# A gated-delta-net layer on one core: the decay matrix from loaded rows, and the products with ones widened from 1 to 64 columns

## The chip, the core and the metric

One core of a Trainium2 chip runs the whole program. The metric is the device time of one execution in microseconds (us). Engines: PE (TensorE) multiplies, DVE (VectorE), ACT (ScalarE) and POOL (GpSimd) do elementwise work, and the queue of SP (SyncE) issues the loop's transfers.

## The reference, cut to what matters

`x` is (8, 1024, 128). A layer norm is followed by an attention-like recurrence over 16 heads, and then by a small feed-forward layer; both are added to `x`.

```
q, k, v = causal_conv_silu(x @ Wq.T), ... ; q, k = l2_norm(q), l2_norm(k)
alpha = exp(-exp(A_log) * softplus(x @ Wa.T + dt_bias));  beta = 2 * sigmoid(x @ Wb.T)
S = alpha_t * (S - beta_t * k_t k_t^T S) + k_t v_t^T;     o_t = S^T q_t     (scan over t)
y = rms_norm(o) @ Wo.T
```

## The kernel before

**Tiling.** The scan is done in chunks of C = 64 positions. One *step* is one pair of heads and one chunk for all 8 batch rows: 8 pairs times 16 chunks, 128 steps. Data of two heads lie on partitions 0 to 63 and 64 to 127, and the 8 rows side by side, so most tiles are 128 x 512. In a chunk, with g the log decay and G its running sum, every product of position t with position j carries the decay exp(G_t - G_j). For one step it stands in `ex` as two 128 x 512 blocks: the one for the Gram matrix of k (multiplied by a column `bn` in `pool_dmn`, L995) and the one for q against k (masked in `pool_dmp`, L999). It is made thus: `pool_lm` (L967) multiplies two triangular masks by g into `Lm`; `pe_dec` (L513) sums them with triangular ones into PSUM; `act_exp` (L726) takes one exponential of 128 x 1024.

**Products with ones.** Three sums over partitions are done on PE with a moving operand of one column: `pe_nk` (L523, squares of k), `pe_nq` (L533, squares of q), `pe_ms` (L696, squares of the output `osq`). PE issues each f32 matmul as two passes, so the trace counts twice as many. In the form column, 64*64 is the part of the array that a pass uses (rows*columns); passes on different parts can run side by side.

**Pipeline.** One turn of the loop works on three steps: n (projections, convolution, decay, Gram matrix), m = n - 1 (inverse of the chunk's triangular system, via DRAM and small blocks), l = n - 2 (output and state). Each engine has its order written by hand (`pe_body`, `act_body`, `dve_body`, `pool_body`, `sp_body`), and semaphores join them. PSUM banks 0 and 1 serve all four projections of a step, so these are a ring: projection on PE (L502), first tap on ACT (L719), three more taps on DVE (L852), then the next projection may start.

**The chain between the second and the third projection.** PE does `pe_gram_p` (L554), `pe_ks` (L626), `pe_dec` (L513), then `pe_ms` (L696), which waits for DVE's PT (L897) because it shares its banks. DVE takes the result in `dve_ro_in` (L881, tile `sc`), PE then does `pe_nk` (L523), DVE `dve_n2` and `dve_r2` (L859, L867), POOL `bn` (L976) and `pool_dmn` (L995), DVE `dve_n` (L890, tile `Nd`), and after that the taps of the third projection (L852). `dve_nqs` (L873) runs once at the end of a step on DVE, so its starts mark the steps.

**Transfers.** SP's queue is in order. In one turn it stores `Nd` to DRAM (`sp_gram`, L1089), waits for these stores, gathers 16 x 16 blocks of it (`sp_gram_in`, L1096, tile `NS`) for POOL's elimination (L1047 and after), and later loads the rows of exp(G) for the query (`sp_g`, L1082, tile `ex`).

Of the kernel before, what the change touches and what calls it, by code (L numbers as in the profile page):

```python
# [14 lines left out]
F32 = mybir.dt.float32  # L15
ALU = mybir.AluOpType
# [23 lines left out]
RESET = -1.0e4  # L40
# [40 lines left out]
def build(nc, x, wtab, wo, wab, hcol, cst, wf, mu, out):  # L81
    with ExitStack() as ctx:
# [18 lines left out]
        Lm = sb("Lm", 2 * 512)  # L101
# [22 lines left out]
        scrG = nc.dram_tensor("scrG", (STEPS, 2, NB * C), F32, kind="Internal").ap()  # L124
        eps = sb("eps", 4)
# [56 lines left out]
        with nc.Block() as block:  # L182
# [32 lines left out]
            def _(dve):  # L215
# [55 lines left out]
                nc.vector.tensor_copy(tp[:, :, 0:8], v8(la))  # L271
                nc.vector.tensor_scalar(tp[:, :, 8:16], v8(be), -1.0, None, ALU.mult)
                dve.wait_ge(cexp.sem, 1)
                nc.vector.scalar_tensor_tensor(tr[:, :, 0:4], v8(tmp[0])[:, :, 0:4], -1.0, v8(be)[:, :, 0:4], ALU.mult, ALU.mult)
                dve.wait_ge(cexp.sem, 2)
                nc.vector.scalar_tensor_tensor(tr[:, :, 4:8], tr[:, :, 4:8], -1.0, v8(be)[:, :, 4:8], ALU.mult, ALU.mult)
# [170 lines left out]
        PB = {"dec": 4, "nk": 2, "gk": 2, "nq": 4, "gp": 2, "ktr": 4, "vtr": 4, "y0": 4, "z0": 4, "x": 2, "y1": 4, "z1": 6, "ks": 6, "u": 2, "o": 2, "ds": 6, "ms": 2, "wo": 6}  # L447
# [635 lines left out]

        def sp_gram(sp, n):
# [552 lines left out]
```

## Time and profile before

| | |
|---|---|
| runs (us) | 3733.55, 3722.45, 3717.49; median 3722.45 |
| profiled execution | span 3725.1 us; no device time beside its span is listed |
| busy: PE, DVE, ACT, POOL | 88%, 70%, 72%, 62% of the span |
| DMA | 28.8% of 16 engines, 61 GB/s |
| mean granted TensorE clock | 0.922 |
| first and last start of L873 | 147.3 and 3505.9 us (128 of them) |
| ahead of the loop: transposes L1379 | 1.95 us for 8 passes, then two PSUM copies L1368 of 0.60 us, then two stores to `scrG` |

The span of the profiled execution lies 2.7 us above the median of the runs. The busy shares are means over the program. The granted clock is given as a share of 2.4 GHz: 1.00 is 2.4 GHz, 0.50 is 1.2 GHz.

### The profile page before, as it was taken

How to read it: one execution, taken by the hardware profiler on the slowest of the kernel's cores; microseconds unless marked ns; L12 is line 12 of the kernel's file. 1: busy time of each engine (PE TensorE's matmuls, PEld its weight loads, DVE VectorE, ACT ScalarE, POOL GpSimd, SP SyncE). 2: the span in 40 equal slices, each digit the busy share in tenths (PEclk: the TensorE clock that was granted, in tenths of full speed). 3: DMA queues.
4: the chain of work that ended last, by engine and by line, in shares of the span. 5: the costliest groups of instructions: out<-in, count | busy, mean ns of one | idle time of the engine just before them, and what ended most of it. 6: DMA issues, size and time to landing. Idle time of an engine off the chain costs nothing. (4 is left out here: it accounts for less than half of the span.)

```text
span 3725.1 us, 195058 instructions
## 1 busy us (share of the span) xinstructions
PE 3292.6 (88%) x77978; PEld 2742.6 (74%) x77978; DVE 2605.8 (70%) x5465; ACT 2677.6 (72%) x5548; POOL 2301.4 (62%) x3558
## 2 busy tenths in 40 slices
PE   5699999999999999999999999999999999999775
PEld 4577777777777777777777777777777777777643
DVE  6677777777777777777777777777777777777453
ACT  2577777777777777777777777777777777777553
POOL 2456666666666666666666666666666666666345
PEclk9789999999999999999999999999999999999777
DMA  2223223232323232323323232323233232323111
GB/s 59 52 61 64 62 62 67 57 67 56 69 56 70 58 66 58 66 59 64 64 60 64 60 67 57 71 57 67 61 63 64 60 65 59 65 59 70 42 34 46
DMA packets 911057, 226.12 MB, mean 61 GB/s; under 512 B 820128, under 2 KB 894112, under 8 KB 911008
## 3 DMA queue, kind: packets, MB, share of 16 engines
q1 hardware_dynamic: 910848, 224.91, 28.8%
q8 instruction: 33, 0.54, 0.1%
q0 software_dynamic: 160, 0.53, 0.0%
q14 instruction: 16, 0.13, 0.0%
HBM read 169.73 MB, written 55.58 MB: 60 GB/s over the span
## 5 line engine op out<-in xcount | busy, mean ns | idle before, releaser
L852 DVE SCALAR_TENSOR_TENSOR cv<-ps,w_kq,cv 128x512 f32<-128x512 f32 x768 | 575.5, 749 | 417.1 <-ACT cv L719 403.5
L852 DVE SCALAR_TENSOR_TENSOR cv<-ps,w_v,cv 128x512 f32<-128x512 f32 x768 | 575.4, 749 | 153.0 <-ACT cv L719 134.9
L1016 POOL TENSOR_TENSOR accT<-accT,X 128x512 f32 (+1 forms) x128 | 163.3, 1276 | 530.2 <-ACT Y L817 530.2
L502 PE MATMUL ps<-xnT,w_kq 128*128 (+1 forms) x1024 | 325.7, 442 | 74.6 <-DVE cv L852 69.0
L502 PE MATMUL ps<-xnT,w_v 128*128 (+1 forms) x1024 | 335.2, 453 | 15.2 <-DVE cv L852 15.0
L1007 POOL TENSOR_TENSOR Sg<-S,tabR 128x512 f32<-128x512 f32 x256 | 333.8, 1323 | 0.0
L976 POOL TENSOR_TENSOR sc<-tabP,sc 128x8 f32<-128x8 f32 x128 | 26.3, 206 | 497.5 <-DVE sc L867 497.5
L765 ACT ACTIVATE Vt<-ps,sc 128x128 f32<-128x128 f32 x1024 | 278.8, 384 | 54.8 <-PE ps L571 54.8
L706 PE MATMUL ps<-wo_s,oo 128*128 128x128 f32 x2048 | 305.6, 309 | 1.2 <-issue 1.2
L967 POOL TENSOR_TENSOR Lm<-k_all,tabP 128x512 f32<-128x512 f32 x256 | 277.2, 1102 | 30.5 <-POOLq L182 30.5
L706 PEld LDWEIGHTS ps<-wo_s,oo 128*128 128x128 f32 x2048 | 280.8, 220 | 14.5 <-issue 1.7
L952 DVE SCALAR_TENSOR_TENSOR Rr<-ps,sc,Vt 128x128 f32<-128x128 f32 x1024 | 288.2, 344 | 1.3
L696 PEld LDWEIGHTS ps<-k_all,KB 128*128 128x128 f32 x2048 | 240.6, 193 | 58.7 <-issue 58.7
L637 PEld LDWEIGHTS ps<-Rr,Z 64*64 64x64 f32 x4096 | 238.1, 141 | 54.5 <-issue 54.5
L502 PEld LDWEIGHTS ps<-xnT,w_kq 128*128 128x128 f32 x1024 | 184.1, 200 | 126.0 <-issue 93.2
L637 PE MATMUL ps<-Rr,Z 64*64 64x128 f32 x4096 | 269.1, 284 | 1.9 <-issue 1.9
L696 PE MATMUL ps<-k_all,KB 128*128 128x1 f32 x2048 | 248.3, 251 | 5.9 <-ACT KB L802 2.1
L585 PEld LDWEIGHTS ps<-Z,NM 64*64 64x64 f32 x8192 | 187.4, 166 | 78.6 <-issue 78.6
L808 ACT ACTIVATE oo<-ps 128x1024 f32<-128x1024 f32 x128 | 131.2, 1025 | 154.3 <-PE ps L653 154.3
L585 PE MATMUL ps<-Z,NM 64*64 64x64 f32 x8192 | 213.2, 255 | 29.2 <-DVE Z L941 28.1
L653 PE MATMUL ps<-PT,U 64*64 64x64 f32 x8192 | 216.7, 221 | 23.8 <-PE ps L650 22.8
L719 ACT ACTIVATE cv<-ps,w_kq 128x512 f32<-128x512 f32 x256 | 174.3, 681 | 74.8 <-PE ps L502 74.7
(197 smaller groups left out, 8542.9 us busy)
## 6 DMA issues: line engine op xcount, KB each, us to landing
ex<-scrG SPq DMA_DIRECT2D x256, 128.0 KB, 2.9
scrN<-Nd SPq DMA_DIRECT2D x256, 128.0 KB, 2.6
Z<-scrZ SPq DMA_DIRECT2D x256, 128.0 KB, 3.2
X<-scrX SPq DMA_DIRECT2D x512, 64.0 KB
w_kq<-wtab SPq DMA_DIRECT2D x128, 132.0 KB, 2.2
w_v<-wtab SPq DMA_DIRECT2D x128, 132.0 KB, 2.5
wo_s<-wo SPq DMA_DIRECT2D x128, 128.0 KB, 2.8
NS<-scrN SPq DMA_DIRECT2D x128, 64.0 KB, 2.6
```

Source lines behind the costliest of these rows:

```text
L502: last = nc.tensor.matmul(pj[:, 4 * g:4 * g + 4, 0:CW], w[:, (j % 2) * P:(j % 2 + 1) * P], xnT3[:, 4 * g:4 * g + 4, bass.ds((n % NC) * C, ...
L585: last = nc.tensor.matmul(ps[place(cls, a), col64(PB["y1" if l else "y0"], cls, i)], blk64(BD["NM"], b, a), blk64(BD["Z"], b, a), start=Tr ...
L637: last = nc.tensor.matmul(ps[a:z, col128(PB["u"], g, i)], blk64(BD["Z"], b, a), unit(Rr, b)[a:z], start=True, stop=True)
L653: last = nc.tensor.matmul(o_cols(h ^ cls, b, d), U[a:z, b * P + d:b * P + d + 64], blk64(BD["PT"], b, a), start=False, stop=(b == NB - 1))
L696: last = nc.tensor.matmul(ps[:, (PB["ms"] + h) * 512 + i:(PB["ms"] + h) * 512 + i + 1], osq[:, h * 512 + i * P:h * 512 + (i + 1) * P], kc( ...
L706: last = nc.tensor.matmul(ps[:, col128(PB["wo"], h, i)], oo[:, h * 512 + i * P:h * 512 + (i + 1) * P], wo_s[:, h * D:(h + 1) * D], start=T ...
L719: nc.scalar.activation(cv4[:, j], pj[:, :, 0:C], ACT.Copy, scale=tap(j, 0)).then_inc(tap0[j].sem, 1)
L765: last = nc.scalar.activation(unit(Vt, b), unit(ps, 4 * PB["vtr"] + b), ACT.Copy, scale=rv[:, b:b + 1])
L852: nc.vector.scalar_tensor_tensor(cv4[:, j], pj[:, :, k:k + C], tap(j, k), cv4[:, j], ALU.mult, ALU.add).then_inc(conv[j].sem, 1)
L952: last = nc.vector.scalar_tensor_tensor(unit(Rr, b), ps[:, col128(PB["ks"], g, i)], cr[:, b:b + 1], unit(Vt, b), ALU.mult, ALU.add)
L967: last = nc.gpsimd.tensor_tensor(v3(Lm, i), over(kc(o, C), NB, C), tabP3[:, bass.ds(n, 1), 0:8].rearrange("p o b -> p b o").to_broadcast([ ...
L1007: nc.gpsimd.tensor_tensor(half(Sg, g).rearrange("p (b v) -> p b v", b=4), half(S, g).rearrange("p (b v) -> p b v", b=4), gam, ALU.mult).th ...
```

## The change

The decay is no longer summed on PE. G itself is kept in `tabP` (rows 0 to 7 of a step) and, transposed, in DRAM (`scrE`, stored once ahead of the loop beside `scrG`). In each turn SP loads the rows G_j, spread over 64 partitions, into `Er` (two transfers of 128 KB, `sp_e`), between `sp_gram` and `sp_gram_in`. POOL subtracts G_t (`pool_df`), ACT takes the absolute value and then exp(-x) of 128 x 512 in `Ee` (`act_abs`, `act_exp`), and POOL makes both blocks of `ex` from the one `Ee`; the masks drop the wrong half as before. The large negative number that cut off the state at a sequence's start is replaced by zeros in the tables `tabR` and `tmp[0]`. The three products with ones move 64 columns (64 equal results, of which the first is read), in blocks of 64 output partitions: `pe_nq` and `pe_ms` become 16 matmuls where they were 8.

```diff
-                la4 = la[:].rearrange("p (h c b) -> p h c b", h=HP, c=NC)
-                nc.vector.memset(la4[0:1, :, 0, :], RESET)
-                then(nc.vector.memset(la4[64:65, :, 0, :], RESET))
...
-        def pe_dec(pe, n):
-            pe.wait_ge(lm_ok.sem, lm_ok.at(n))
-            pe.sem_inc(pe_go.sem, 1)
-            for i, o in enumerate((K_LE, K_GT)):
-                for cls in range(2):
-                    for a, z in HALF:
-                        c = (PB["dec"] + cls) * 512 + i * 4 * C
-                        last = nc.tensor.matmul(ps[place(cls, a), c:c + 4 * C], k_all[a:z, o + a:o + z],
-                                                Lm[a:z, i * 512 + cls * 4 * C:i * 512 + (cls + 1) * 4 * C], start=True, stop=True)
-            last.then_inc(dec_mm.sem, 1)
-
         def pe_nk(pe, n):
             pe.wait_ge(sq_k.sem, sq_k.at(n))
             pe.sem_inc(pe_go.sem, 1)
             for i in range(4):
                 for cls in range(2):
                     for a, z in HALF:
-                        last = nc.tensor.matmul(ps[place(cls, a), (PB["nk"] + cls) * 512 + i:(PB["nk"] + cls) * 512 + i + 1],
-                                                blk64(sq_kt, CLASSES[cls][i], a), k_all[a:z, K_BD + a:K_BD + a + 1],
-                                                start=True, stop=True)
+                        last = nc.tensor.matmul(ps[place(cls, a), col64(PB["nk"], cls, i)], blk64(sq_kt, CLASSES[cls][i], a),
+                                                k_all[a:z, K_BD + a:K_BD + z], start=True, stop=True)
...
-                    last = nc.tensor.matmul(ps[:, (PB["nq"] + h) * 512 + i:(PB["nq"] + h) * 512 + i + 1],
-                                            sq_qt[a:z, i * P:(i + 1) * P], k_all[a:z, K_BD + a:K_BD + a + 1], start=True, stop=True)
+                    for e, (c, d) in enumerate(HALF):
+                        last = nc.tensor.matmul(ps[c:d, col64(PB["nq"], h, i)], blk64(sq_qt, 2 * i + e, a),
+                                                k_all[a:z, K_BD + a:K_BD + z], start=True, stop=True)
...
-            for h in range(2):
-                for i in range(4):
-                    last = nc.tensor.matmul(ps[:, (PB["ms"] + h) * 512 + i:(PB["ms"] + h) * 512 + i + 1],
-                                            osq[:, h * 512 + i * P:h * 512 + (i + 1) * P], kc(K_ONE, 1), start=True, stop=True)
+            for i in range(4):
+                for h in range(2):
+                    for e, (c, d) in enumerate(HALF):
+                        o = h * 512 + (2 * i + e) * C
+                        last = nc.tensor.matmul(ps[c:d, col64(PB["ms"], h, i)], osq[:, o:o + C], kc(K_ONE, C), start=True, stop=True)
...
+        def act_abs(act, n):
+            act.wait_ge(df_ok.sem, df_ok.at(n))
+            if not first(n):
+                act.wait_ge(dmn_ok.sem, dmn_ok.at(n - 1))
+                act.wait_ge(dmp_ok.sem, dmp_ok.at(n - 1))
+            nc.scalar.activation(Ee[:], Er[:], ACT.Abs).then_inc(ab_ok.sem, 1)
+
         def act_exp(act, n):
-            act.wait_ge(dec_mm.sem, dec_mm.at(n))
-            if not first(n):
-                act.wait_ge(nd_ok.sem, nd_ok.at(n - 1))
-                act.wait_ge(pt_ok.sem, pt_ok.at(n - 1))
-            nc.scalar.activation(ex[:, 0:1024].rearrange("p (i g n) -> p g i n", i=2, g=2),
-                                 bank(PB["dec"], 2).rearrange("p (g i n) -> p g i n", g=2, i=2), ACT.Exp).then_inc(dec_ex.sem, 1)
+            act.wait_ge(ab_ok.sem, ab_ok.at(n))
+            nc.scalar.activation(Ee[:], Ee[:], ACT.Exp, scale=-1.0).then_inc(dec_ex.sem, 1)
...
-        def pool_lm(pool, n):
-            if not first(n):
-                pool.wait_ge(dec_mm.sem, dec_mm.at(n - 1))
+        def pool_df(pool, n):
+            pool.wait_ge(e_in.sem, e_in.at(n))
             pool.sem_inc(pool_go.sem, 1)
-            for i, o in enumerate((K_MGT, K_MLE)):
-                last = nc.gpsimd.tensor_tensor(v3(Lm, i), over(kc(o, C), NB, C),
-                                               tabP3[:, bass.ds(n, 1), 0:8].rearrange("p o b -> p b o").to_broadcast([P, NB, C]), ALU.mult)
-            last.then_inc(lm_ok.sem, 1)
+            nc.gpsimd.tensor_tensor(v3(Er, 0), v3(Er, 0), tabP3[:, bass.ds(n, 1), 0:8].rearrange("p o b -> p b o").to_broadcast([P, NB, C]),
+                                    ALU.subtract).then_inc(df_ok.sem, 1)
...
-            nc.gpsimd.tensor_tensor(v3(ex, 0), v3(ex, 0), bcast(bn, C), ALU.mult).then_inc(dmn_ok.sem, 1)
+            if not first(n):
+                pool.wait_ge(nd_ok.sem, nd_ok.at(n - 1))
+            nc.gpsimd.tensor_tensor(v3(ex, 0), v3(Ee, 0), bcast(bn, C), ALU.mult).then_inc(dmn_ok.sem, 1)
 
         def pool_dmp(pool, n):
             pool.wait_ge(dec_ex.sem, dec_ex.at(n))
-            nc.gpsimd.tensor_tensor(v3(ex, 1), v3(ex, 1), over(kc(K_MLE, C), NB, C), ALU.mult).then_inc(dmp_ok.sem, 1)
+            if not first(n):
+                pool.wait_ge(pt_ok.sem, pt_ok.at(n - 1))
+            nc.gpsimd.tensor_tensor(v3(ex, 1), v3(Ee, 0), over(kc(K_MLE, C), NB, C), ALU.mult).then_inc(dmp_ok.sem, 1)
 
         def pool_sg(pool, m):
...
+        def sp_e(sp, n):
+            if not first(n):
+                sp.wait_ge(ab_ok.sem, ab_ok.at(n - 1))
+            sp.sem_inc(sp_go.sem, 1)
+            for h, (a, z) in enumerate(HALF):
+                sp.dma_start(Er[a:z], scrE[bass.ds(n, 1), h, :].to_broadcast([C, NB * C])).then_inc(e_in.sem, 16)
...
+            for k in range(4):
+                sp.wait_ge(g_cp.sem, g_cp.at(0, k + 1))
+                sp.dma_start((scrG, scrE)[k // 2][:, k % 2, :], half((U, Rr)[k // 2], k % 2)).then_inc(g_out.sem, 16)
...
                 sp_gram(sp, m)
+            if n is not None:
+                sp_e(sp, n)
+            if m is not None:
                 sp_gram_in(sp, m)
                 sp_z_out(sp, m)
             if l is not None:
...
-            if n is not None:
-                if m is not None:
-                    pe.wait_ge(kt_ok.sem, kt_ok.at(m))
-                pe_dec(pe, n)
...
-                if n is not None:
-                    pe.wait_ge(dec_ex.sem, dec_ex.at(n))
-                else:
-                    pe.wait_ge(kt_ok.sem, kt_ok.at(m))
```

PE's rows in one turn of the loop, from the second projection on (Lm, KB = `osq`, sq are the tiles of `pe_dec`, `pe_ms`, `pe_nk`). Before:

```order
105 L502 MATMUL ps<-xnT,w_kq 128x4x67 x2
106 L564 MATMUL ps<-k_all,sl 64x64 x16
107 L554 MATMUL ps<-sl 64x64 x16
108 L626 MATMUL ps<-S,sl 64x128 x16
109 L507 REGISTER_ALU
110 L513 MATMUL ps<-Lm,k_all 64x256 x8
111 L696 MATMUL ps<-k_all,KB 128x1 x8
112 L523 MATMUL ps<-k_all,sq 64x1 x16
```

Of the change, from the Gram product (`pe_gram_p`) on:

```order
116 L544 MATMUL ps<-sl 64x64 [waits silu_q,osq_ok,silu_k]
117 L544 MATMUL ps<-sl 64x64 x15
118 L616 MATMUL ps<-S,sl 64x128 [waits s1_ok,silu_k,s0_ok]
119 L616 MATMUL ps<-S,sl 64x128 x15
120 L688 MATMUL ps<-k_all,KB 64x64 [waits pt_ok,osq_ok]
121 L688 MATMUL ps<-k_all,KB 64x64 x15
122 L513 MATMUL ps<-k_all,sq 64x64 [waits ro_in,sq_k]
123 L513 MATMUL ps<-k_all,sq 64x64 x15
```

The eight matmuls of 256 columns are gone; `pe_ms` follows `pe_ks`, still behind the wait for PT.

SP's queue in one turn, around the stores of `Nd`. Before:

```order
57 L1063 DMA w_kq<-wtab 128x264
58 L1089 DMA scrN<-Nd 64x8x64 [waits n_in,nd_ok]
59 L1089 DMA scrN<-Nd 64x8x64
60 L1092 ISA
61 L1094 ISA [waits n_out]
62 L1095 ISA [waits elim]
63 L1096 DMA NS<-scrN 64x16x16 [waits sub]
```

Of the change:

```order
63 L1091 DMA scrN<-Nd 64x8x64 [waits n_in,nd_ok]
64 L1091 DMA scrN<-Nd 64x8x64
65 L1084 ISA [waits ab_ok]
66 L1084 DMA Er<-scrE 64x512
67 L1084 ISA
68 L1084 DMA Er<-scrE 64x512
69 L1094 ISA
70 L1096 ISA [waits n_out]
71 L1097 ISA [waits elim]
72 L1098 DMA NS<-scrN 64x16x16 [waits sub]
```

Two issues for `Er` stand between the stores and the wait for them, behind a wait for ACT's absolute value of the step before.

## Rows read from the trace of the kernel before

**Rows 1.** Timeline of DVE, its row L873 at the end of four steps:

```profile
start us, us, engine line op out<-in xcount [idle before <-releaser]
1528.39 0.15 DVE L873 TENSOR_SCALAR sc<-ps 128x8 f32<-128x8 f32 x1
1554.75 0.16 DVE L873 TENSOR_SCALAR sc<-ps 128x8 f32<-128x8 f32 x1
1582.67 0.16 DVE L873 TENSOR_SCALAR sc<-ps 128x8 f32<-128x8 f32 x1
1607.87 0.16 DVE L873 TENSOR_SCALAR sc<-ps 128x8 f32<-128x8 f32 x1
```

**Rows 2.** Windows of these three steps (PEclk: granted clock, then DMA share):

```profile
1528.40:1554.75 26.35, 24.25 (x604) 20.73 (x600) 19.32 (x39) 19.97 (x42) 17.43 (x29) 0.94 0.32 63
1554.75:1582.67 27.92, 25.82 (x604) 21.50 (x600) 19.32 (x38) 20.09 (x42) 17.08 (x27) 0.88 0.28 59
1582.67:1607.87 25.20, 22.79 (x604) 19.28 (x600) 18.96 (x39) 20.09 (x42) 16.53 (x25) 1.00 0.32 65
```

**Rows 3.** Windows before and in two falls of the clock:

```profile
1514.60:1517.80 3.20, 2.85 (x54) 2.74 (x51) 2.42 (x8) 2.77 (x3) 1.07 (x2) 1.00 0.58 160
1517.80:1521.20 3.40, 3.40 (x69) 2.49 (x67) 2.15 (x9) 2.51 (x6) 2.58 (x4) 0.51 0.47 105
1551.90:1555.40 3.50, 2.67 (x109) 2.41 (x101) 2.32 (x4) 2.08 (x5) 2.64 (x8) 1.00 0.19 18
1555.40:1558.80 3.40, 3.40 (x18) 2.49 (x20) 0.61 (x1) 2.05 (x4) 2.93 (x9) 0.50 0.00 0
```

**Rows 4.** Timeline of PE just before these two falls:

```profile
1514.60 1.95 PE L696 MATMUL ps<-k_all,KB 128*128 128x1 f32 x16
...
1553.11 1.06 PE L533 MATMUL ps<-k_all,sq 64*128 64x1 f32 x16 [0.33 <-ACT Y L780]
```

**Rows 5.** Timeline of PE in a step at full clock:

```profile
2016.09 0.69 PE L554 MATMUL ps<-sl 64*64 64x64 f32 x32 [0.41 <-ACT KB L802]
...
2017.45 1.07 PE L513 MATMUL ps<-Lm,k_all 64*64 64x256 f32 x16
2018.58 1.92 PE L696 MATMUL ps<-k_all,KB 128*128 128x1 f32 x16
2020.84 0.64 PE L523 MATMUL ps<-k_all,sq 64*64 64x1 f32 x32 [0.35 <-DVE sc L881]
```

**Rows 6.** Timeline of DVE in the same step:

```profile
2017.75 0.68 DVE L897 TENSOR_TENSOR PT<-ps,ex 128x512 f32<-128x512 f32 x1
2018.35 1.53 DVE L852 SCALAR_TENSOR_TENSOR cv<-ps,w_kq,cv 128x512 f32<-128x512 f32 x2
2020.53 0.17 DVE L881 TENSOR_TENSOR sc<-ps,sc 128x8 f32<-128x8 f32 x1 [0.65 <-PE ps L696]
...
2023.91 0.69 DVE L890 TENSOR_TENSOR Nd<-ps,ex 128x512 f32<-128x512 f32 x1 [0.67 <-POOL ex L995]
2024.52 2.31 DVE L852 SCALAR_TENSOR_TENSOR cv<-ps,w_v,cv 128x512 f32<-128x512 f32 x3
```

**Rows 7.** Timeline of ACT in the same step:

```profile
2018.46 0.63 ACT L742 ACTIVATE sq<-sl 128x512 f32<-128x512 f32 x1
...
2020.41 1.02 ACT L726 ACTIVATE ex<-ps 128x1024 f32<-128x1024 f32 x1
2021.94 0.21 ACT L825 ACTIVATE sc<-sc 128x8 f32<-128x8 f32 x1 [0.51 <-DVE sc L859]
...
2028.25 0.69 ACT L719 ACTIVATE cv<-ps,w_v 128x512 f32<-128x512 f32 x1 [0.24 <-PE ps L502]
```

**Rows 8.** Timeline of PE, the forms nearest to the new products:

```profile
14.15 1.94 PE L322 MATMUL ps<-k_all,PT 128*128 128x128 f32 x8 [14.15 <-DVE PT L240]
...
21.71 3.60 PE L329 MATMUL ps<-cv,xnT 128*64 128x16 f32 x64
...
2009.55 1.09 PE L571 MATMUL ps<-k_all,sv 128*128 128x128 f32 x8
```

**Rows 9.** Waits of SP's queue (total us, times, longest), and one DMA group:

```profile
SPq L1094 <- DMA scrN<-Nd: 236.8, 124, 1.9
...
ex<-scrG SPq DMA_DIRECT2D x256, 128.0 KB, 2.9
```

More of the change, by code:

```diff
@@ L39 @@
 HALF = ((0, 64), (64, 128))
-RESET = -1.0e4
 EPS_LN = 1e-5
@@ L100, in build @@
         sc = sb("sc", 64)
-        Lm = sb("Lm", 2 * 512)
+        Er = sb("Er", 512)
+        Ee = sb("Ee", 512)
         ex = sb("ex", 3 * 512)
@@ L124, in build @@
         scrG = nc.dram_tensor("scrG", (STEPS, 2, NB * C), F32, kind="Internal").ap()
+        scrE = nc.dram_tensor("scrE", (STEPS, 2, NB * C), F32, kind="Internal").ap()
         eps = sb("eps", 4)
@@ L270, in _ @@
                 v8 = lambda t: t[:].rearrange("p (n k) -> p n k", k=8)
-                nc.vector.tensor_copy(tp[:, :, 0:8], v8(la))
                 nc.vector.tensor_scalar(tp[:, :, 8:16], v8(be), -1.0, None, ALU.mult)
-                dve.wait_ge(cexp.sem, 1)
+                dve.wait_ge(cexp.sem, 2)
+                nc.vector.tensor_copy(tp[:, :, 0:4], bank(0, 2).rearrange("p (n k) -> p n k", k=8)[:, :, 0:4])
+                nc.vector.tensor_copy(tp[:, :, 4:8], bank(6).rearrange("p (n k) -> p n k", k=4))
                 nc.vector.scalar_tensor_tensor(tr[:, :, 0:4], v8(tmp[0])[:, :, 0:4], -1.0, v8(be)[:, :, 0:4], ALU.mult, ALU.mult)
-                dve.wait_ge(cexp.sem, 2)
-                nc.vector.scalar_tensor_tensor(tr[:, :, 4:8], tr[:, :, 4:8], -1.0, v8(be)[:, :, 4:8], ALU.mult, ALU.mult)
+                then(nc.vector.scalar_tensor_tensor(tr[:, :, 4:8], tr[:, :, 4:8], -1.0, v8(be)[:, :, 4:8], ALU.mult, ALU.mult))
+                nc.vector.memset(tabR[:].rearrange("p (h c k) -> p h c k", h=HP, c=NC)[:, :, 0, :], 0.0)
+                nc.vector.memset(tmp[0][:].rearrange("p (h c b) -> p h c b", h=HP, c=NC)[:, :, 0, :], 0.0)
                 then(nc.vector.memset(S[:], 0.0))
@@ L353, in build @@
         g_tr = sig("g_tr")
-        g_cp = sig("g_cp", 2)
-        g_out = sig("g_out", 32)
+        g_cp = sig("g_cp", 4)
+        g_out = sig("g_out", 64)
         g_in = sig("g_in", 32)
-        lm_ok = sig("lm_ok")
-        dec_mm = sig("dec_mm")
+        e_in = sig("e_in", 32)
+        df_ok = sig("df_ok")
+        ab_ok = sig("ab_ok")
         dec_ex = sig("dec_ex")
@@ L445, in build @@
         acc3 = accT[:].rearrange("p (c k) -> p c k", k=512)
-        PB = {"dec": 4, "nk": 2, "gk": 2, "nq": 4, "gp": 2, "ktr": 4, "vtr": 4, "y0": 4, "z0": 4, "x": 2, "y1": 4, "z1": 6, "ks": 6, "u": 2, "o": 2, "ds": 6, "ms": 2, "wo": 6}
+        PB = {"nk": 2, "gk": 2, "nq": 4, "gp": 2, "ktr": 4, "vtr": 4, "y0": 4, "z0": 4, "x": 2, "y1": 4, "z1": 6, "ks": 6, "u": 2, "o": 2, "ds": 6, "ms": 2, "wo": 6}
         def tap(j, k):
@@ L481, in tiny @@
         def tiny(bk):
-            return bank(bk, 2).rearrange("p (g n) -> p g n", g=2)[:, :, 0:4]
+            return bank(bk, 2).rearrange("p (g i c) -> p g i c", g=2, c=C)[:, :, 0:4, 0]
         def two(t):
@@ L1126, in sp_start @@
         def sp_start(sp):
-            for h, n in enumerate(("X", "Y")):
-                sp.wait_ge(g_cp.sem, g_cp.at(0, h + 1))
-                sp.dma_start(scrG[:, h, :], half(BD[n], 1)).then_inc(g_out.sem, 16)
+            for k in range(4):
+                sp.wait_ge(g_cp.sem, g_cp.at(0, k + 1))
+                sp.dma_start((scrG, scrE)[k // 2][:, k % 2, :], half((U, Rr)[k // 2], k % 2)).then_inc(g_out.sem, 16)
             sp.wait_ge(g_out.sem, g_out.at(0))
@@ L1165, in pe_body @@
                 else:
-                    pe.wait_ge(dec_ex.sem, dec_ex.at(m))
+                    pe.wait_ge(nd_ok.sem, nd_ok.at(m))
                 pe_vtr(pe, m)
@@ L1261, in act_body @@
             if n is not None:
+                act_abs(act, n)
                 act_exp(act, n)
@@ L1321, in pool_body @@
             if n is not None:
-                pool_lm(pool, n)
+                pool_df(pool, n)
             if m is not None:
@@ L1366, in _ @@
                 act.wait_ge(g_tr.sem, g_tr.at(0))
-                for h, n in enumerate(("X", "Y")):
-                    nc.scalar.activation(v3(BD[n], 1), bank(4, 2).rearrange("p (b h t) -> p b h t", b=NB, h=2)[:, :, h, :],
+                for k in range(4):
+                    nc.scalar.activation(v3((U, Rr)[k // 2], k % 2),
+                                         bank(4 + k // 2 * 2, 2).rearrange("p (b h t) -> p b h t", b=NB, h=2)[:, :, k % 2, :],
                                          ACT.Copy).then_inc(g_cp.sem, 1)
@@ L1378, in _ @@
                 for b in range(NB):
-                    last = nc.tensor.transpose(unit(ps, 16 + b), tmp[0][:].rearrange("p (n b) -> p n b", b=NB)[:, :, b], ident)
+                    nc.tensor.transpose(unit(ps, 16 + b), tmp[0][:].rearrange("p (n b) -> p n b", b=NB)[:, :, b], ident)
+                for b in range(NB):
+                    last = nc.tensor.transpose(unit(ps, 24 + b), tabP[:].rearrange("p (n k) -> p n k", k=24)[:, :, b], ident)
                 last.then_inc(g_tr.sem, 1)
```

## The prediction

> **What bounds the kernel now.** I read first the page with its row of granted clock, then the starts of one instruction that runs once a step, then windows of single steps, and last the timelines of PE, DVE and ACT through one step.
>
> The steps come in three lengths. The starts in [rows 1] are 26.36, 27.92 and 25.20 us apart, and the windows of the same three steps [rows 2] hold the same instructions on PE (604 each) at a mean granted clock of 0.94, 0.88 and 1.00. So one step at the full clock takes 25.20 us; one in which the clock falls once takes some 1.2 us more, one in which it falls twice 2.7 us more. Over the loop, L873 goes from 147.3 to 3505.9 us in 127 intervals, 26.45 us each. Against 127 steps of 25.20 (3200.4 us) the falls cost 158 us: they are the largest single item that a change could take away.
>
> What does PE do before a fall? In [rows 3] the windows before both falls have PE busy for 2.85 of 3.20 us and 2.67 of 3.50 us at the full clock of 2.4 GHz; the windows after them stand at 0.51 and 0.50, which is 1.2 GHz. PE was not idle. But [rows 4] show its work there: before the first fall `pe_ms`, 16 passes of one column in 1.95 us (with `pe_nk`, 32 passes of one column, behind it), before the second `pe_nq`, 16 passes of one column in 1.06 us. These are the places in a step in which PE loads weights and moves almost no columns.
>
> Within a step at full clock the order is set by the ring of projections. Between the second and the third projection it runs through PT, `pe_ms`, `sc` on DVE, `pe_nk`, the two small DVE operations, POOL's `bn` and `pool_dmn`, `Nd`, and the third projection's taps [rows 5, 6]: `Nd` starts 0.67 us after DVE fell idle, released by POOL's L995, and the taps start at its end.
>
> **The change, part by part.**
>
> `pe_dec` goes: 16 passes, 1.07 us [rows 5]. I cost this at nothing. It ends at 2018.52; `pe_ms` behind it also waits for PT, which ends at 2018.43 [rows 6]. PE will wait for PT instead. Without that cover it would be worth its 1.07 us.
>
> `pe_ms` becomes 32 passes of half the width with 64 columns. No row shows this form at full clock. From below: 32 passes of 64*64 with 64 columns take 0.69 us [rows 5], but four of them fit side by side, and here only two. From above: 64 passes of the same part of the array (128*64) with 16 columns take 3.60 us [rows 8], 56 ns each, so 32 take 1.80 us. That row lies in a stage where eight full passes take 1.94 us; the same shape takes 1.09 us in the loop [rows 8], so I read that stage as the lower clock, whatever its row of clock says. Twice the 64*64 passes' steady rate, or half of the 1.80 us, and a tail of some 0.2 us: I take 1.15 us, a gain of 0.77 on 1.92.
>
> Not all of it arrives. DVE reads the result (L881) only after two taps that end at 2018.35 + 1.53 = 2019.88; today it starts at 2020.53 [rows 6]. So `sc`, `pe_nk`, `bn`, `Nd` and the taps can move ahead by 0.65 at most. On ACT one exponential of 1.02 us becomes two passes over half the elements, 0.63 us and some 0.02 between them, by the square of the same size [rows 7]: 1.28 us, so 0.26 more. Today ACT then idles 0.51 us for DVE [rows 7]. It will idle no more, and what is behind it, up to the last first tap (L719 at 2028.25), moves ahead by 0.51 - 0.26 = 0.25. That tap waits 0.24 for PE today; PE will be ahead, so this wait goes too. **The step gains about 0.46 us**, set by ACT, of 0.65 that DVE would allow. With 1.80 us for `pe_ms` it gains 0.12; with 0.69 still 0.46.
>
> `pe_nk` keeps 32 passes; 0.64 us with one column against 0.69 with 64 [rows 5], plus 0.05, inside the estimate. `pe_nq` goes from 16 passes in 1.06 us [rows 4] to 32 of 64*64, 0.69 us; the third set of taps sets the next step's first projection, so I cost the 0.37 at nothing.
>
> POOL does one operation where it did two, ahead of a wait for DVE; nothing. SP issues two more transfers of 128 KB between the stores and the gather. SP waits 1.9 us per step there for the stores (236.8 us in 124 times), and a load of this kind lands 2.9 us after its issue [rows 9]; the rows are wanted almost a turn later by POOL's first operation. I cost it at nothing; the bound is 2.9 - 1.9 = 1.0 us by which the gather behind it could be late, and then POOL's elimination, `Sg` and DVE's `S`. The wait for ACT's absolute value is over long before `Nd` is ready, so nothing queued behind it (gather, `scrZ`, weights) is held.
>
> Ahead of the loop: eight more transposes (1.95 us), two more copies of 0.60, two more stores: 5 us.
>
> **The clock.** The one-column passes are what PE did before the falls, and after the change none is left: `pe_ms`, `pe_nk` and `pe_nq` move 64 columns in each of 32 passes. On the other side 16 passes of 256 columns go with `pe_dec`, and an idle stretch of about 0.9 us stands in its place. Counting pass by pass over the stretch from `pe_dec` to `pe_nk`, columns go from 16 x 256 + 48 to 64 x 64: as many as before, but now spread over the stretch in which there were none. I take it that no falls are left. The bounds: falls as today, or more of them.
>
> The Trainium skill speaks against this. "TensorE: Matmul & The Clock Gate", section "Why this matters for your kernels", names idle gaps between bursts of matmuls as what sends the clock down. The trace disagrees: before the falls PE was busy nine and eight tenths [rows 3]. By that rule widened columns change nothing and the new gap can only harm: the first and the third rival below.
>
> **The sum**, against the span: 127 x (25.20 - 0.46) = 3142 us where 3358.6 stood, so 3725.1 - 216.6 + 5 = 3513.5. The median of the runs lies 2.7 below the span: **3510 us**, 5.7% faster. Own range 3475 to 3560, from a step of 24.5 to 25.1.
>
> **Rivals.**
>
> *The falls stay as they are.* For it: what makes the clock fall I infer from two places and their columns. Then only 0.46 per step is gained: 3722.5 - 58 + 5 = 3669 us; with half of them left 3590. Chance 0.12 together.
>
> *The gather is late.* For it: DMA is busiest around the stores. Against it: the wait of 1.9 us at that very place. At the full 1.0 us a step, 3510 + 127 = 3637 us. Chance 0.07.
>
> *More falls: slower.* If what counts is the columns that `pe_dec` moved, or the gap, every step could fall twice, at 27.92 - 0.46 = 27.46 us: 3722.5 + 129 + 5 = 3856 us. It decides from a mean fall cost of 1.7 us a step (today 1.25). Chance 0.05.
>
> *The two halves of `pe_ms` don't overlap.* They use the same rows of the array. If each pass costs what a full one does (1.92 / 16 = 120 ns, [rows 5]), 32 take 3.84 us and the step 27.1: 3810 us; at half of that, 3569. Against it stand the 56 ns of L329 at the lower clock [rows 8]. Chance 0.02. The Trainium skill ("TensorE: Matmul & The Clock Gate", "Part 3: Packing small matmuls — row/col tiling") says that weight loads overlap running matmuls only where row groups differ, which would make this the likely case; L329 alternates halves on the same rows and doesn't bear it out.
>
> A mixture that ends within 0.5% of no change (about what a measurement of this kernel can tell) gets the remaining 0.02. So faster 0.91, same 0.02, slower 0.07. The range 3465 to 3670 takes in the first case, the late gather and most of the first rival.
>
> **What would show it.** Right: starts of `dve_nqs` evenly 24.7 us apart; a granted clock of 1.00 through the loop; `pe_ms` in about 1.15 us, starting right after PT with about 0.9 us of PE idle before it; ACT without idle time before the logarithm. Wrong: windows at 0.5 in the loop; POOL waiting longer for `NS`, or DVE's `S` for `Sg`; `pe_ms` over 1.8 us.

## The result, and the profile after

| | before | after |
|---|---|---|
| median of the runs beside each other | 3726.48 us (3717.49 to 3733.55) | 3496.06 us (3493.49 to 3499.48) |
| ratio | | 0.938, 95% interval 0.936 to 0.940 |
| span of the profiled execution | 3725.1 | 3493.8 |
| first and last step mark on DVE | 147.3, 3505.9 | 150.8, 3274.4 |
| mean of the 127 intervals | 26.45 | 24.60 |

The change makes the kernel 6.2% faster. From the page of the changed kernel, the span, the granted clock in 40 slices, and the group of `pe_ms`:

```profile
span 3493.8 us, 199678 instructions
PEclk9699999999999999999999999999999999999777
L688 PE MATMUL ps<-k_all,KB 128*64 128x64 f32 x4096 | 150.0, 226 | 114.6 <-DVE PT L891 112.4
```

PE now idles 114.6 us ahead of `pe_ms`, nearly all of it for DVE's PT: 0.90 us per step where `pe_dec` stood. One window of 700 us in the middle of the loop, columns as in [rows 2]:

```profile
1000.00:1700.00 700.00, 590.86 (x17576) 495.57 (x17567) 544.05 (x1064) 574.92 (x1229) 462.02 (x738) 1.00 0.37 79
```

and the same window of the kernel before:

```profile
1000.00:1700.00 700.00, 642.15 (x15956) 541.37 (x15960) 507.49 (x977) 530.42 (x1113) 458.81 (x723) 0.94 0.30 62
```

The clock stands at 1.00. Every engine but PE is busier in the same 700 us, because more steps fit into them; PE is less busy. `dve_nqs` is now L867, and its marks, at places that answer to [rows 1], are 24.47 us apart:

```profile
2021.46 0.15 DVE L867 TENSOR_SCALAR sc<-ps 128x8 f32<-128x8 f32 x1
2045.93 0.15 DVE L867 TENSOR_SCALAR sc<-ps 128x8 f32<-128x8 f32 x1
```

Between 1000 and 1700 us nearly every interval is 24.47 to 24.49 (25 of 27). Timeline of PE through the changed stretch, to be read against [rows 5], with `pe_nq` (L523, in [rows 4] L533):

```profile
2007.54 1.08 PE L616 MATMUL ps<-S,sl 64*64 64x128 f32 x32
2009.53 1.15 PE L688 MATMUL ps<-k_all,KB 128*64 128x64 f32 x32 [0.90 <-DVE PT L891]
2011.14 0.69 PE L513 MATMUL ps<-k_all,sq 64*64 64x64 f32 x32 [0.47 <-DVE sc L875]
...
2020.16 0.70 PE L523 MATMUL ps<-k_all,sq 64*64 64x64 f32 x32 [0.33 <-ACT Y L774]
2020.64 0.68 PE L601 MATMUL ps<-Y,X 64*64 64x64 f32 x32
2021.99 1.17 PE L503 MATMUL ps<-xnT,w_kq 128*128 x4 [0.68 <-DVE cv L846]
```

`pe_ms` takes 1.15 us. DVE in the same step, for [rows 6]:

```profile
2008.70 0.68 DVE L891 TENSOR_TENSOR PT<-ps,ex 128x512 f32<-128x512 f32 x1
2009.30 1.53 DVE L846 SCALAR_TENSOR_TENSOR cv<-ps,w_kq,cv 128x512 f32<-128x512 f32 x2
2010.74 0.15 DVE L875 TENSOR_TENSOR sc<-ps,sc 128x8 f32<-128x8 f32 x1
...
2014.08 0.69 DVE L884 TENSOR_TENSOR Nd<-ps,ex 128x512 f32<-128x512 f32 x1 [0.66 <-POOL ex L988]
```

From the start of `pe_ms` to the start of `Nd` it was 5.33 us in [rows 5, 6] and is 4.55 here: 0.78 came off. And ACT, for [rows 7]:

```profile
2011.46 0.63 ACT L717 ACTIVATE Ee<-Er 128x512 f32<-128x512 f32 x1
2012.12 0.63 ACT L721 ACTIVATE Ee<-Ee 128x512 f32<-128x512 f32 x1
2012.66 0.19 ACT L819 ACTIVATE sc<-sc 128x8 f32<-128x8 f32 x1
...
2018.49 0.69 ACT L710 ACTIVATE cv<-ps,w_v 128x512 f32<-128x512 f32 x1
```

The absolute value and the exponential end at 2012.75, and the logarithm (L819) follows with no idle time. The last first tap (L710) no longer waits for PE.

One sign that the prediction called wrong did appear: POOL waits longer for `NS`. Its wait before, then in the change:

```profile
POOL XT L1047 <- DMA NS<-scrN: 72.3, 70, 7.9
POOL XT L1042 <- DMA NS<-scrN: 162.9, 128, 6.7
```

DVE's `S` waits for `Sg` 22.1 us in 123 times, where it was 6.5 in 36. The experiments show below that the row loads are not the cause of either.

### The profile page after: what moved, and what is told of

Its sections match the earlier page's. It is cut to its first block and busy times, and to the rows that moved or that the text cites. A ratio compares the mean times of both kernels' runs of the same rounds, so it can differ in the third digit from the quotient of the medians.

```text
span 3493.8 us, 199678 instructions
## 1 busy us (share of the span) xinstructions
PE 2849.6 (82%) x80034; PEld 2361.8 (68%) x80034; DVE 2587.6 (74%) x5466; ACT 2686.5 (77%) x5678; POOL 2173.0 (62%) x3430
## 5 line engine op out<-in xcount | busy, mean ns | idle before, releaser
L1002 POOL TENSOR_TENSOR Sg<-S,tabR 128x512 f32<-128x512 f32 x256 | 408.2, 1613 | 0.0
L503 PE MATMUL ps<-xnT,w_kq 128*128 (+1 forms) x1024 | 305.6, 420 | 97.2 <-DVE cv L846 90.0
L503 PE MATMUL ps<-xnT,w_v 128*128 (+1 forms) x1024 | 305.3, 420 | 3.6 <-DVE cv L846 3.5
L503 PEld LDWEIGHTS ps<-xnT,w_kq 128*128 128x128 f32 x1024 | 174.9, 191 | 145.5 <-issue 115.8
L697 PE MATMUL ps<-wo_s,oo 128*128 128x128 f32 x2048 | 263.2, 282 | 1.3 <-DVE Rr L946 1.3
L697 PEld LDWEIGHTS ps<-wo_s,oo 128*128 128x128 f32 x2048 | 239.3, 192 | 9.9 <-issue 1.4
L688 PE MATMUL ps<-k_all,KB 128*64 128x64 f32 x4096 | 150.0, 226 | 114.6 <-DVE PT L891 112.4
L601 PE MATMUL ps<-Y,X 64*64 64x64 f32 x8192 | 176.0, 221 | 75.3 <-ACT Y L774 66.6
L710 ACT ACTIVATE cv<-ps,w_kq 128x512 f32<-128x512 f32 x256 | 174.0, 680 | 75.3 <-PE ps L503 75.2
L688 PEld LDWEIGHTS ps<-k_all,KB 128*64 128x64 f32 x4096 | 135.9, 140 | 141.9 <-issue 141.9
L1045 POOL TENSOR_TENSOR tmpE<-NS,XT 64x24 f32<-64x24 f32 (+3 forms) x768 | 186.6, 243 | 60.4
L601 PEld LDWEIGHTS ps<-Y,X 64*64 64x64 f32 x8192 | 151.3, 135 | 96.2 <-issue 96.1
```

The lines of the kernel that those rows point to most:

```text
L503: last = nc.tensor.matmul(pj[:, 4 * g:4 * g + 4, 0:CW], w[:, (j % 2) * P:(j % 2 + 1) * P], xnT3[:, 4 * g:4 * g + 4, bass.ds((n % NC) * C, ...
L601: last = nc.tensor.matmul(ps[a:z, col64(PB["z1" if l else "z0"], cls, i)], BD["X" if l else "X0"][q, b * C:(b + 1) * C], BD["Y"][q, b * C: ...
L688: last = nc.tensor.matmul(ps[c:d, col64(PB["ms"], h, i)], osq[:, o:o + C], kc(K_ONE, C), start=True, stop=True)
L697: last = nc.tensor.matmul(ps[:, col128(PB["wo"], h, i)], oo[:, h * 512 + i * P:h * 512 + (i + 1) * P], wo_s[:, h * D:(h + 1) * D], start=T ...
L710: nc.scalar.activation(cv4[:, j], pj[:, :, 0:C], ACT.Copy, scale=tap(j, 0)).then_inc(tap0[j].sem, 1)
L1002: nc.gpsimd.tensor_tensor(half(Sg, g).rearrange("p (b v) -> p b v", b=4), half(S, g).rearrange("p (b v) -> p b v", b=4), gam, ALU.mult).th ...
```

## The experiments

Each ran beside the kernel before on the same chip, whose median there was 3724.8 to 3728.6 us. The ratios are against it, with their 95% intervals. The step lengths are those of the window 1000 to 1700 us. Where a row names another line for an operation, the edit shifted it.

### The theories

Mine: what sends the clock down is that PE moves almost no columns there, and widening takes the falls away. The first rival: it is idle gaps. The second: it is the form of the passes (full width against halves), not the columns. The third: the gain lies in the loaded rows and the work that they take off POOL and PE.

### One column again, loaded rows kept

```diff
-   (16 matmuls in halves, 64 columns, in pe_nq and pe_ms; 64 columns in pe_nk)
+   last = nc.tensor.matmul(ps[:, p:p + 1], osq[:, h * 512 + i * P:h * 512 + (i + 1) * P], kc(K_ONE, 1), ...)
```

(`pe_nk` and `pe_nq` likewise in their old form.)

> The changed kernel with the three products with ones back at one column and in their old shape (8 + 8 matmuls for the output's and the query's squares, 16 for the key's); the decay from loaded rows stays. Columns theory: the granted clock falls again at the places of the one-column passes, the steps spread again over lengths 1.1 to 2.8 us apart above some 25.2 us, and the run takes 3690 to 3800 us, since the 4096 columns of the old decay products are missing as well. Rival, that the time came from dropping the decay's matmuls and its chain through PE: the steps stay near 24.5 us, 3480 to 3530 us.

Measured: 3843.9 us (3837.0 to 3855.1), ratio 1.033 (1.029 to 1.036). With the loaded rows alone the kernel is slower than before, by more than I expected. The steps are 25.2 (once in the window), 26.4 to 26.5, 27.7 and 28.0 us long, 27.1 in the mean. Two windows in it, before a fall and in the fall:

```profile
1526.40:1532.30 5.90, 4.54 (x100) 3.82 (x96) 5.16 (x15) 4.76 (x10) 1.16 (x3) 1.00 0.60 141
1532.30:1536.10 3.80, 3.80 (x66) 3.68 (x58) 3.05 (x5) 2.85 (x4) 2.49 (x4) 0.55 0.48 111
```

The first window holds `pe_ms` with one column, `pe_nk` with one column, and the gap of 0.91 us before them. So `pe_dec` did keep the clock up in part of the steps: taking its 16 passes of 256 columns away, with a gap in their place, makes falls more frequent. Whether its columns or its busy time did this, no run tells apart. That is the mechanism of my slower rival. The gap of about 0.9 us is present both here and in the changed kernel, whose clock stays at 1.00, so the gap by itself doesn't bring a fall; in the changed kernel the wider products make up for what `pe_dec` moved.

### Widened products alone, `pe_dec` kept

```diff
-   ps[:, (PB["ms"] + h) * 512 + i:... + i + 1], osq[:, ...128 wide...], kc(K_ONE, 1)
+   ps[c:d, col64(PB["ms"], h, i)], osq[:, o:o + C], kc(K_ONE, C)        # pe_nk, pe_nq alike, in before
```

> The kernel before with only the three products widened to 64 columns in blocks of 64 rows; the decay still comes from matmuls on PE and one exponential of 128 x 1024. Columns theory: no falls of the clock in the loop, steps of one length between 24.3 and 24.8 us, 3480 to 3530 us, so that the loaded rows bring nothing by themselves (the decay's matmuls lie beside the wait for PT). Rival, that the loaded rows carry part of the gain: 3580 us or more.

Measured: 3527.5 us (3524.2 to 3528.9), ratio 0.946 (0.944 to 0.949); clock 1.00 in the window, steps 24.71 to 24.97, mean 24.80. So the widening alone brings 200 of some 231 us. The other 31 need the loaded rows: the time lies in my range, but that the loaded rows bring nothing doesn't hold. The timeline of this kernel shows what they take away:

```profile
1904.01 1.08 PE L626 MATMUL ps<-S,sl 64*64 64x128 f32 x32
1905.38 1.09 PE L513 MATMUL ps<-Lm,k_all 64*64 64x256 f32 x16 [0.28 <-POOL Lm L968]
1906.40 1.15 PE L698 MATMUL ps<-k_all,KB 128*64 128x64 f32 x32
```

`pe_dec` waits for POOL, which makes `Lm` in two operations (19.4 us of such waits over the loop). Before, L513 started 0.87 or 0.88 us after L626 (1594.11 against 1593.23, and 2017.45 against 2016.58); here, in the 28 steps of the window, it starts 1.13 to 1.50 after it. So `pe_ms` starts 2.16 to 2.52 us after L626, mean 2.30, against 1.99 in the changed kernel. That is 0.31 of the 0.32 us by which the steps differ. In 8 of these steps PE also waits some 0.4 us for `X`, but they are no longer than the others.

This kernel has no row loads, and yet POOL waits for the gather and DVE for `Sg` (22.0 us in 123 times) as long as in the change, or longer:

```profile
POOL XT L1048 <- DMA NS<-scrN: 212.3, 128, 6.5
```

And the kernel of the section before, which has the row loads and steps of 27.1 us, has only 37.9 us of that wait in 54 times. So the waits come with the shorter step, not with the loads.

### `pe_ms` in full width: 64 columns, then 128

```diff
+   last = nc.tensor.matmul(ps[:, p:p + C], osq[:, h * 512 + i * P:h * 512 + (i + 1) * P], kc(K_ONE, C), ...)      # 8 matmuls
```

> The changed kernel with the output's squares summed in the old shape (8 matmuls of 128 output rows) but with 64 columns each. It takes the split into halves away and keeps the columns. If columns hold the clock and the split shortens this product: clock at 1.00 through the loop, the product back near 1.95 us instead of 1.15, steps of 25.1 to 25.3 us, 3570 to 3600 us. Rival, that the length of this product is off the path: 3490 to 3505 us.

Measured: 3645.0 us (3643.8 to 3653.2), ratio 0.979 (0.976 to 0.981). I missed: the falls were not gone. The steps without a fall take 25.22 us; about half take 26.4 to 26.6. A fall in it begins right after this:

```profile
1508.48 1.97 PE L687 MATMUL ps<-k_all,KB 128*128 128x64 f32 x16 [0.90 <-DVE PT L891]
1510.90 0.75 PE L513 MATMUL ps<-k_all,sq 64*64 64x64 f32 x32 [0.45 <-DVE sc L875]
1511.59 2.15 PE L503 MATMUL ps<-xnT,w_v 128*128 x4
```

L503 takes 2.15 us where it takes 1.18 at the full clock. These 16 passes of 64 columns carry half the columns of the 32 of the changed kernel, in 1.97 us where those take 1.15. Two readings were left: too few columns, or the full width itself. The same 8 matmuls with 128 columns tell them apart:

> The changed kernel with the output's squares in the old shape (8 matmuls of 128 output rows) and 128 columns each instead of 64. With 64 columns in this shape the clock still fell in about half of the steps. Theory: what PE moves in this stretch decides, and 16 passes of 64 columns were half of what the changed kernel's 32 passes move; with 128 columns the falls go, the product takes about 2.05 us, all steps take 25.2 to 25.4 us, 3580 to 3610 us. Rival, that the full-width shape itself lets the clock fall: falls as with 64 columns, 3640 us or more.

Measured: 3595.2 us (3592.6 to 3597.9), ratio 0.965 (0.964 to 0.967). The windows from 1000 to 1700 us of the two kernels, with 64 columns and then with 128:

```profile
1000.00:1700.00 700.00, 601.65 (x16300) 504.27 (x16300) 521.13 (x1006) 552.87 (x1173) 438.20 (x703) 0.97 0.35 74
1000.00:1700.00 700.00, 597.34 (x16608) 502.66 (x16612) 529.79 (x1029) 565.30 (x1189) 446.89 (x713) 1.00 0.36 76
```

Every step takes 25.25 to 25.32 with 128 columns. `pe_ms` takes 2.02 us where it took 1.97, behind the same gap of 0.90 us, and the falls are gone. Form, gap and duration are the same or nearly so; only the number of columns differs, so here it decides whether the clock stays up. The halves give the shorter time besides: 25.28 - 24.48 = 0.80 us per step.

### The new form with one column, and with 16

```diff
-   ps[c:d, col64(PB["ms"], h, i)], osq[:, o:o + C], kc(K_ONE, C)
+   ps[c:d, p:p + 1], osq[:, o:o + C], kc(K_ONE, 1)                      # likewise pe_nk, pe_nq; then with 16
```

> The changed kernel with all three products in the new shape (blocks of 64 output rows) but with one column each. The short product stays (near 1.1 us), the columns go. Columns theory: the clock falls as in the kernel before or more, 3600 to 3720 us: slower than the changed kernel by 100 us or more, faster than the same with the old shape. Rival, that the shape alone brought the gain: 3490 to 3510 us.

Measured: 3837.3 us (3832.8 to 3842.7), ratio 1.030 (1.027 to 1.034). Every step is 27.2 to 27.4 us long, and in the step looked at the clock falls twice, near 1504 and 1517.7 us. The mean clock of the window:

```profile
1000.00:1700.00 700.00, 606.23 (x15830) 511.38 (x15832) 489.41 (x951) 515.58 (x1102) 414.16 (x664) 0.87 0.33 70
```

I expected a shorter time, 3720 us at most; the direction is clear. The form alone gains nothing: with the halves kept, the columns are worth 341 us.

> The changed kernel with the three products in the new shape and 16 columns each, between 1 and 64. Columns theory with a graded effect of how many columns PE moves: fewer falls than with one column but not none, a time between that run and the changed kernel, 3510 to 3650 us. Rival, that a product needs only to be in the new shape or to move more than one column: 3490 to 3505 us.

Measured: 3537.2 us (3536.0 to 3542.2), ratio 0.949 (0.946 to 0.953). Most steps take 24.48 us, and every third or fourth 25.7:

```profile
1000.00:1700.00 700.00, 592.19 (x17343) 497.56 (x17336) 536.26 (x1047) 567.40 (x1214) 456.14 (x733) 0.98 0.36 77
```

Falls become rarer as columns are added: with one column, 16 and 64 they come in the order foreseen.

### `pe_nq` alone with one column: old form, then halves

```diff
+   last = nc.tensor.matmul(ps[:, o:o + 1], sq_qt[a:z, i * P:(i + 1) * P], k_all[a:z, K_BD + a:K_BD + a + 1], ...)
```

> The changed kernel with the query's squares alone back at 8 matmuls of one column. Columns theory with a fall at each starved place: some steps have a fall right after this product, as the second of the two falls shown of the kernel before; at most one step in three, 3510 to 3600 us. Rival, that only the longer starved place (output's and key's squares) matters: no falls, 3490 to 3505 us.

Measured: 3622.5 us (3614.5 to 3628.9), ratio 0.971 (0.969 to 0.974). Steps alternate between 24.73 and 26.35 us: a fall in about every second step, where I expected one in three at most and 3600 us at most. Timeline of PE at a fall of this kernel:

```profile
1561.03 1.06 PE L523 MATMUL ps<-k_all,sq 64*128 64x1 f32 x16 [0.33 <-ACT Y L774]
1562.02 0.69 PE L601 MATMUL ps<-Y,X 64*64 64x64 f32 x32
1563.15 1.98 PE L503 MATMUL ps<-xnT,w_kq 128*128 x4 [0.44 <-issue]
```

and its windows before and in the fall:

```profile
1560.00:1563.30 3.30, 2.53 (x97) 2.27 (x89) 2.32 (x4) 1.65 (x5) 1.97 (x6) 1.00 0.26 35
1563.30:1567.10 3.80, 3.80 (x26) 2.90 (x28) 1.10 (x2) 2.16 (x5) 3.17 (x10) 0.55 0.00 0
```

This is the second place of [rows 4], by itself. The run shows something else too. Steps without a fall are 24.73 here and 24.48 in the changed kernel. L503 starts with "issue" (a delay for which the profile shows no wait), not after a wait for DVE's taps: PE's own order, `pe_nq`, L601 and the turn of the loop, now sets the step, and the 0.36 us that the new form saves on `pe_nq` is worth 0.25.

> The changed kernel with the query's squares in the new shape (16 matmuls, blocks of 64 output rows) but with one column each. With the old shape and one column the steps without a fall took 24.73 us instead of 24.48. If the shape of this product made that difference and its columns the falls: 24.48 us in steps without a fall, a fall in about half of the steps, 3570 to 3610 us. Rival, that the falls come with the old shape: 3490 to 3505 us.

Measured: 3499.4 us (3496.6 to 3506.5), ratio 0.939 (0.937 to 0.942); clock 1.00, steps 24.48 to 24.97, mean 24.56. I expected falls, and my rival was right:

```profile
1579.13 0.64 PE L524 MATMUL ps<-k_all,sq 64*64 64x1 f32 x32 [0.33 <-ACT Y L775]
1579.59 0.70 PE L602 MATMUL ps<-Y,X 64*64 64x64 f32 x32
1580.97 1.17 PE L503 MATMUL ps<-xnT,w_kq 128*128 x4 [0.68 <-DVE cv L847]
```

One column in halves takes 0.64 us instead of 1.06, and the clock holds. A product with one column is not by itself what brings a fall: the two kernels differ in the stretch that it takes and in its form. When all three products have one column in halves, though, this same place does fall, as that kernel's timeline shows:

```profile
1515.40 0.64 PE L525 MATMUL ps<-k_all,sq 64*64 64x1 f32 x32 [0.33 <-ACT Y L777]
1515.86 0.70 PE L603 MATMUL ps<-Y,X 64*64 64x64 f32 x32
1517.58 2.10 PE L503 MATMUL ps<-xnT,w_kq 128*128 x4 [1.01 <-DVE cv L849]
```

The first two rows are the same, the idle time behind them is longer, 1.01 against 0.68 us, and this kernel has another fall earlier in the same step. Which of these two makes the difference is not settled, and so the columns of one product alone don't tell whether the clock falls behind it.

### The row loads behind the gather

```diff
-                sp_e(sp, n)
                 sp_gram_in(sp, m)
+                sp_e(sp, n)
```

> The changed kernel with the two row transfers issued behind the gather instead of ahead of it. Rows theory (they are hidden): the gather is issued up to 0.1 us earlier, DVE may stop waiting 0.18 us for POOL's scaled state, and the run stays at 3490 to 3500 us. Rival, that the rows hold the gather back and the gather sets the step: 0.2 to 0.5 us less per step, 3430 to 3475 us.

Measured: 3494.6 us (3490.8 to 3499.5), ratio 0.938 (0.935 to 0.941), the same as the change; steps 24.48. The waits of the two kernels agree, the changed one's first:

```profile
POOL XT L1042 <- DMA NS<-scrN: 162.9, 128, 6.7
```

and with the loads behind the gather:

```profile
POOL XT L1042 <- DMA NS<-scrN: 154.5, 128, 6.6
```

POOL waits 0.07 us less per step for the gather, and the end doesn't notice. SP's own wait for the stores of `Nd` is 47.9 us in 124 times in the changed kernel, where it was 236.8 [rows 9]: the two loads are issued in time that SP spent waiting before.

### The sign by a mask on POOL instead of ACT's absolute value

ACT stood without idle time before the logarithm, so I took its absolute value away. POOL multiplies by a constant tile of signs (1 and -1) instead, and ACT takes exp(Er) once.

```diff
+            nc.gpsimd.tensor_tensor(v3(Er, 0), v3(Er, 0), over(Sn[:], NB, C), ALU.mult).then_inc(ab_ok.sem, 1)
-            nc.scalar.activation(Ee[:], Er[:], ACT.Abs).then_inc(ab_ok.sem, 1)
-            nc.scalar.activation(Ee[:], Ee[:], ACT.Exp, scale=-1.0).then_inc(dec_ex.sem, 1)
+            nc.scalar.activation(Ee[:], Er[:], ACT.Exp).then_inc(dec_ex.sem, 1)
```

> The changed kernel with the absolute value replaced by a multiplication with a sign mask on POOL, so that ACT does one pass of 128 x 512 for the decay instead of two. If ACT sets the third and fourth first taps, as I argued: ACT's work behind it moves 0.65 us ahead, of which the chain through Nd lets 0.2 to 0.5 us through, 3430 to 3475 us. Rival, that the step is set by the chain through Nd or by POOL: 3490 to 3505 us, or slower if POOL's added 1.0 us delays its next operations.

Measured: 3542.9 us (3537.2 to 3547.9), ratio 0.951 (0.947 to 0.954): slower than the change by 47 us, and a miss: I expected 3430 to 3475 or, by the rival, 3490 to 3505 or slower. The steps vary from 24.4 to 25.4 us. Its waits:

```profile
PE ps L603 <- DMA X<-scrX: 121.4, 125, 2.7
POOL XT L1044 <- DMA NS<-scrN: 276.8, 128, 7.8
```

Its queue on SP shows a wait that the changed kernel doesn't have:

```profile
SPq L1077 <- POOL QG L1026: 81.8, 122, 0.7
```

POOL's extra operation (1.28 us) delays its QG, which frees `ex` for `sp_g` (L1077), and the loads of `X` stand behind `sp_g` in SP's in-order queue. The next two runs move `sp_g` behind the gather, one turn later in SP's order: with the sign on POOL, and by itself.

```diff
                 sp_gram_in(sp, m)
+                sp_g(sp, m)
                 sp_z_out(sp, m)
...
-                sp_g(sp, n)
```

> The kernel with the sign mask on POOL, and the query's exp(G) rows now loaded one turn later in SP's queue, behind the gather, so that the four loads of X0 are issued some 1.4 us earlier. Theory: the sign mask was slower because PE then waits 1 us a step for these loads (121.4 us in 125 times); with them early the shorter work on ACT shows, steps of 24.2 to 24.4 us, 3455 to 3490 us. Rival, that POOL's second operation and its pressure on the shared path make it slow: it stays near 3540 us.

> The changed kernel with only that move in SP's queue. Theory: PE waits for ACT's Y there and not for X0, so nothing changes, 3490 to 3500 us. Rival, that the loads are late in the changed kernel too: 3440 to 3480 us.

Measured over five executions each: with the sign on POOL 3480.3 us (3479.0 to 3482.4), ratio 0.934 (0.932 to 0.936), steps 24.41; the move alone 3493.1 us (3491.5 to 3493.6), ratio 0.937 (0.936 to 0.939), steps 24.48. PE's wait for `X` is gone and POOL's for the gather falls:

```profile
POOL XT L1044 <- DMA NS<-scrN: 190.2, 128, 7.4
```

The first is the fastest kernel of the study. It beats the move alone by 12.8 us or 0.37%; the two don't overlap. That is below the 0.5% that I set as distinguishable, so I give it as a small gain at most. Taking ACT's second pass away, with one more operation on POOL, is worth 0.07 us in a step (24.48 to 24.41).

## Why the prediction was right, and where its sizes were off

The forecast was 3510 us, and 3496 was measured. Most of the gain is where it was placed. That the number came this close is in part luck, since two errors have opposite signs: against the span, 3493.8 instead of 3513.5, the clean step gave 33 us more than forecast, and the falls 15 us less.

**The falls.** Forecast: all gone, 158 us; gone they are, and worth 144 (see below). In the loop the clock is 1.00, and steps are even. That columns are the cause is shown by four kernels: with the changed form and one column the kernel takes 3837 us, with 16 columns 3537, and with `pe_ms` in full width it falls in half of the steps at 64 columns and in none at 128. What is not settled is how one stretch adds to another: `pe_nq` with one column is followed by a fall in one kernel and not in the other. The rival of idle gaps, as the prediction took it, falls: there is a new gap of 0.90 us in every step (L688), and the clock stays at 1.00. By the rule cited in the prediction from the Trainium skill ("TensorE: Matmul & The Clock Gate", "Why this matters for your kernels"), as the prediction applied it, the widening would have changed nothing and the falls would have stayed; they went. The other rule cited there from the Trainium skill (the same page, "Part 3: Packing small matmuls — row/col tiling"), that weight loads overlap running matmuls only where row groups differ, isn't borne out by this trace either: 32 passes in 1.15 us are 36 ns each, against 120 ns for a full one [rows 5] or 60 for half of one.

**The clean step.** Forecast 24.74 us, measured 24.48. In the loop this makes 127 x 0.26 = 33 us. Three terms of the sum were mis-sized:

- The gain from `pe_ms`: 0.77 was forecast for the passes (1.92 to 1.15) and came exactly; as the 1.15 was chosen between 0.69 and 1.80, with no row of this form at full clock, this too is partly luck. The caps on what arrives were too tight. DVE's was 0.65, from two taps whose listed time I added up to 2019.88; but DVE's operations overlap in the listing (L875 starts at 2010.74, before 2009.30 + 1.53), and 0.78 came through to `Nd`. ACT's logarithm came 0.23 us nearer to the start of `pe_ms`, where I had 0.25 (2012.66 - 2009.53 = 3.13, against 2021.94 - 2018.58 = 3.36). But its last first tap came 0.71 nearer (8.96 against 9.67 in [rows 5, 7]), where I let through 0.46. (The two terms of that cap, 0.25 and 0.24, add up to 0.49; the sum of the prediction has 0.46, which is 0.03 x 127 = 4 us too little.) So the cap of 0.46 was too low. That ACT does not set the step by much is shown by the run with the sign on POOL: without its second pass the step is 0.07 shorter.
- `pe_nq`: I costed its 0.37 us at nothing, since the third taps set the next projection. After the other gains that wait had shrunk to the point where PE's own order came last; the shortening is worth 0.25, the difference between the steps without a fall of that run and the change.
- `pe_dec` and `pool_lm`: costed at nothing, since PT was due at the same moment. That held for the schedule of before. In the shorter step POOL's two operations are late, and removing them is worth 0.32 (24.80 against 24.48).

These overlap and don't simply add. What the widening alone leaves is 25.20 - 24.80 = 0.40 us of the 0.72 per clean step.

**Against it.** The prologue cost 3.5 us (150.8 against 147.3), where 5 was forecast. At both ends of the loop the steps are longer than in its middle: 27.35, 30.72 and 25.41 us the first three, 26.82 and 26.70 the last two, 14.6 us in all above five of 24.48. In the kernel before they were 29.15, 31.38, 29.44 and 29.12, 27.55, and I had counted all that lies above 25.20 as falls. So the 158 us contain some 15 that are no falls: 234.9 us saved in the loop are 127 x 0.72 = 91 from the clean step and 144 from the falls. After the loop the time is 219 us in both.

**The transfers.** Costed at nothing, with a bound of 1.0 us a step. Moving them behind the gather changed nothing, so the rival of the late gather falls. POOL's longer wait for `NS`, and DVE's for `Sg`, were named as signs of it; both appeared, but they appear as well in the kernel that has the widening and no row loads (212.3 and 22.0 us). As signs of a late gather they were badly chosen: in a shorter step POOL and DVE arrive earlier and wait longer.

**More falls, slower.** It had 0.05 for its condition. The condition is real: without the widening the loaded rows make the kernel 3.3% slower. The forecast rested on the columns of the three products making up for those of `pe_dec`, and they did.

## What to carry to other kernels

When the granted clock dips, look at the passes of PE ahead of the dip before looking for idle time: many weight loads with one moving column each can be a cause (not every such stretch was followed by a dip here), and wider results that nobody reads can cost next to nothing, 0.05 to 0.1 us here, and return more than they take. Before taking a product off PE, ask whether it keeps the clock up; the same edit was 3% slower alone and part of 6% faster with the widening. A term that is free because something else is due at the same moment stays free only until that something moves, so in a sum that takes much off a step every "hidden" neighbour deserves a second look at the new length.

## What the runs showed of the hardware beyond that

- Nearly all of the lost clock reaches the step. In the kernel with `pe_nq` in its old form, 3.80 us at a clock of 0.55 are 3.80 x 0.45 = 1.71 us of full-speed time lost, and the step is 1.62 us longer (26.35 against 24.73).
- 32 passes of 128*64 with 64 columns take 1.15 us (36 ns each), 16 of 128*128 with 64 columns 1.97, and with 128 columns 2.02: in full width the second 64 columns are nearly free. With 16 columns the 32 half-width passes take 1.11 us, with one column 1.10.
- 32 passes of 64*64 take 0.64 us with one column and 0.69 or 0.70 with 64.
